# Scanning the products of later retention gates block by block in the recurrence, before the spill

## The chip, the core and the metric

The kernel runs on one core of one Trainium2 chip. The metric is the device time of one execution in microseconds (us). Engines are named as in the profile: PE (TensorE), ACT (ScalarE), DVE (VectorE), POOL (GpSimd) and SP (SyncE, which here only issues DMAs).

## The reference

The input x has 16 batches of 512 time steps and 512 features, all in float32. Four layers are applied in turn, each as `x = x + layer(x)`.

```python
# layer 0: a Haar transform with every coefficient multiplied by the same gate, undone again
gate = sigmoid(silu(cond @ W1.T + b1) @ W2.T + b2)      # [16, 512], from the conditioning input
x = x + (x + x * gate)                                  # what the transform comes to
# layer 1: recurrence over the 512 steps
xw = x @ Wx + b
h[t] = tanh(xw[t] + h[t-1] @ Wh)
x = x + h
# layer 2: gated scan; h0 is the initial hidden state
f, i = sigmoid(x @ W_f.T + b_f), sigmoid(x @ W_i.T + b_i)
g = f / (f + i + EPS) + EPS                             # retention
n = i / (f + i + EPS) * (x @ W_h.T + b_h)               # new information
scaling[t] = g[t] * g[t+1] * ... * g[511]
hidden[t] = sum_{s<=t} scaling[s] * n[s] + g[0] * ... * g[t] * h0
x = x + hidden
# layer 3: a layer of its own for each batch, from the conditioning input
layer[b] = base_layer + x_a[b] @ x_b[b].T               # rank 8
x = x + (x + x @ layer[b])
```

## The kernel before

Features lie on the 128 partitions in four chunks m = 0..3. The kernel has three phases.

**Preamble, 0 to 32 us.** Weights are loaded and split into high and low parts, and the gate of layer 0 and the first block's input products are made.

**Recurrence, 32 to 1103 us.** The 512 steps form 16 blocks j of 32 steps t; a block holds all 16 batches (a tile of 128 x 512 is a chunk of 16 batches x 32 steps). In each step PE multiplies the hidden state by Wh (`step`, L509: 32 matmuls of 128x32 from `hs`, high and low, into the PSUM tile `sums`, which the profile calls recb; the two halves of a sum lie beside each other). DVE adds the halves (L1480, `pre`), ACT takes tanh of `pre` three times (L763 into the fp16 `hs`, L764 into PSUM `konst`, L767 into `hbuf`), and DVE writes the low part of `hs` (L1492), on which the next step of PE waits. Ahead of PE's next accumulation `seed` (L1335, DVE) puts xw of the next step into `sums`: times 1 in one half, times 0 in the other.

Between two steps PE does six matmuls (L545) of the groups: the input product of the next block ("x"), and the gates f, i and the candidate c of the block before. What the other engines do beside the steps is written in tables by step t: `ACT_WORK`, `DVE_EARLY` (between `pre` and the low part of `hs`) and `DVE_LATE` (behind it); in the last block the tables run four steps ahead. In them "x" is the writing of xw (L779), "g" is `forget_share` (L814, retention g into `gst`), "r" a reciprocal of 128x64 (L1295), "p" a forward scan of g (L1325, two halves of 128x264 for a chunk), and "n" the new information into `nst` (L1306). SP spills g (`g_d`), n (`n_d`) and x (`x2_d`) of each block and chunk to HBM, 256 KB each, because the next phase wants them by batch. POOL adds h to x (L1053, L1055) and the share of the initial state (`add_P`, L1068), and divides the gates.

**Tail, 1103 to 1366 us.** First the gate groups of the last block. Then 64 slots k, four chunks m for each batch b. In a slot DVE scans g backwards over the 512 steps (`suffix`, L1527: the scaling), POOL multiplies n by it (`times_n`, L1160), DVE sums that (`hidden`, L1536) and adds it to x (L1539), ACT takes the high part of x (L961) and POOL the low part (`x3_low`, L1167), and PE multiplies them by the base layer (L734). Once a batch PE makes the rank-8 products (L716), ACT takes their high part (L969, L972), POOL the low part (`y_low`, L1172), PE applies them (L749), ACT writes the output rows (`put_out`, L980) and SP stores them. Each engine works through its list in program order; semaphores alone tie them. SP loads g, n and x of a batch two batches ahead, each in halves of 512 KB.

## Time and profile before

| | us |
|---|---|
| median of 3 runs (lowest, highest) | 1370.43 (1368.74, 1372.99) |
| the profiled execution's own time | 1372.59 |
| its span, first to last instruction | 1370.7 |
| steps of the recurrence (511 rows of L1480) | 32.8 to 1102.3 |
| busy PE / DVE / ACT / POOL | 1340.4 / 1066.7 / 695.2 / 767.2 |

The profile lists each instruction with the engine, the line of the kernel, the time it took and the idle time of its engine just before, with what ended it. A slice of the page is a fortieth of the span, 34 us. An engine's busy share says little by itself; the idle time in front of an instruction, and what released it, tell which engine sets the pace at that place.

### The profile page before, as it was taken

The page shows a single profiled execution, that of the slowest core. Times are in us where ns is not written, and L with a number is a line of the kernel's source. Part 1 is how long each engine was busy: PE and PEld are TensorE (multiplying, and loading weights), DVE is VectorE, ACT ScalarE, POOL GpSimd, SP SyncE. Part 2 cuts the span into 40 slices and gives each one's busy share as a digit, 9 for nine tenths or more (in the row PEclk, how much of TensorE's full clock was granted, in tenths as well). Part 3 has the DMA queues.
Part 4 walks back from the last instruction along what each step waited for, and adds up shares of the span by engine and source line. Part 5 has one row for each costly group of instructions (what it writes and reads, how often), then busy time and mean ns, then how long its engine had stood idle before and what let it go on. Part 6 is the DMA issues. An engine that isn't in the chain of part 4 may idle for free. (4 is left out here: it accounts for less than half of the span.)

```text
span 1370.7 us, 50350 instructions
## 1 busy us (share of the span) xinstructions
PE 1340.4 (98%) x21246; PEld 887.3 (65%) x21246; DVE 1066.7 (78%) x2912; ACT 695.2 (51%) x2228; POOL 767.2 (56%) x620
## 2 busy tenths in 40 slices
PE   8999999999999999999999999999999997999998
PEld 6656666666666666666666666666666644677776
DVE  5756878777777777777777787878777888998993
ACT  4388555555555555555555555555545442333332
POOL 3255655464646464545555555554535557887884
PEclk9999999999999999999999999999999998999999
DMA  9771333333434242424242424241416568999993
GB/s 374 271 264 37 64 65 64 64 64 68 69 63 71 57 78 55 74 56 72 56 80 54 81 49 80 48 72 26 71 25 119 143 146 167 330 325 335 329 323 119
DMA packets 442276, 168.13 MB, mean 123 GB/s; under 512 B 406449, under 2 KB 409649, under 8 KB 438850
## 3 DMA queue, kind: packets, MB, share of 16 engines
q1 hardware_dynamic: 441584, 164.53, 47.6%
q8 instruction: 167, 2.74, 0.8%
q14 instruction: 59, 0.48, 0.1%
q10 hardware_dynamic: 466, 0.38, 0.1%
HBM read 96.72 MB, written 68.16 MB: 120 GB/s over the span
## 5 line engine op out<-in xcount | busy, mean ns | idle before, releaser
L509 PEld LDWEIGHTS recb<-hs,scanS 128*128 128x128 f16 x16352 | 466.1, 96 | 148.2 <-DVE hs L1492 144.3
L509 PE MATMUL recb<-hs,scanS 128*128 128x32 f16 x16352 | 488.3, 176 | 4.6 <-DVE hs L1492 3.5
L763 ACT ACTIVATE hs<-pre 128x64 f16<-128x64 f32 x512 | 131.2, 256 | 489.0 <-DVE pre L1480 487.5
L1480 DVE TENSOR_REDUCE pre<-recb 128x64 f32<-128x128 f32 x511 | 148.9, 291 | 186.4 <-PE recb L509 184.3
L1295 DVE RECIPROCAL gates<-gates 128x64 f32<-128x64 f32 (+1 forms) x484 | 257.8, 555 | 0.4
L1053 POOL TENSOR_SCALAR hbuf<-hbuf,sup 128x512 f32<-128x512 f32 (+2 forms) x61 | 94.1, 1542 | 126.9 <-ACT hbuf L767 126.9
L1492 DVE TENSOR_TENSOR hs<-konst,hs 128x64 f16<-128x64 f32 x512 | 103.5, 202 | 61.5 <-ACT konst L764 49.5
L1068 POOL TENSOR_TENSOR xt<-xt,pout 128x512 f32<-128x512 f32 x64 | 75.5, 1179 | 126.4 <-DVE pout L1325 126.4
L1335 DVE TENSOR_TENSOR recb<-xw,recb 128x128 f32<-128x128 f32 x511 | 145.8, 285 | 0.1
L1061 POOL TENSOR_TENSOR gates<-gates 128x512 f32<-128x512 f32 x62 | 78.8, 1271 | 105.0 <-DVE gates L1295 103.7
L767 ACT ACTIVATE hbuf<-pre 128x64 f32<-128x64 f32 x512 | 122.5, 239 | 0.0
L1036 POOL TENSOR_TENSOR x1l<-xt,x1h 128x512 f16<-128x512 f32 x56 | 64.7, 1159 | 93.8 <-ACT x1h L773 93.8
L1055 POOL TENSOR_TENSOR xt<-xt,hbuf 128x512 f32<-128x512 f32 (+1 forms) x65 | 97.9, 1506 | 25.8 <-DVE ratio L1269 17.3
L1167 POOL TENSOR_TENSOR x3l<-xt,x3h 128x512 fp32r<-128x512 f32 x64 | 82.7, 1294 | 45.6 <-ACT x3h L961 42.9
L764 ACT ACTIVATE konst<-pre 128x64 f32<-128x64 f32 x512 | 107.0, 209 | 0.0
L734 PE MATMUL bank<-wx_hi,x3h 128*128 128x512 f32 x208 | 85.5, 411 | 8.0 <-issue 5.1
L545 PE MATMUL bank<-x2l,wc_h 128*128 128x512 f16 x240 | 90.8, 378 | 0.0
L545 PE MATMUL bank<-x2l,wi_h 128*128 128x512 f16 x240 | 90.8, 378 | 0.0
L545 PE MATMUL bank<-x2h,wi_l 128*128 128x512 f16 x240 | 90.7, 378 | 0.0
L545 PE MATMUL bank<-x2h,wc_l 128*128 128x512 f16 x240 | 90.7, 378 | 0.0
L545 PE MATMUL bank<-x2h,wf_l 128*128 128x512 f16 x240 | 90.7, 378 | 0.0
L545 PE MATMUL bank<-x2h,wf_h 128*128 128x512 f16 x240 | 90.5, 377 | 0.0
(252 smaller groups left out, 2725.7 us busy)
## 6 DMA issues: line engine op xcount, KB each, us to landing
xt<-in_x SPq DMA_DIRECT2D x64, 256.0 KB, 3.5
g_d<-gst SPq DMA_DIRECT2D x64, 256.0 KB, 4.2
n_d<-nst SPq DMA_DIRECT2D x64, 256.0 KB, 3.1
x_d<-xt SPq DMA_DIRECT2D x64, 256.0 KB, 3.3
out<-gates SPq DMA_DIRECT2D x63, 256.0 KB, 4.9
xt<-x_d SPq DMA_DIRECT2D x28, 512.0 KB, 6.1
stage<-in_w SPq DMA_DIRECT2D x11, 1024.0 KB, 6.8
xt<-g_d SPq DMA_DIRECT2D x14, 512.0 KB, 8.0
```

Source lines behind the costliest of these rows:

```text
L509: last = nc.tensor.matmul(sums[t % 2][:, m].rearrange("p a b -> p (a b)"), w[:, k, m * P:(m + 1) * P], hs[:, k].rearrange("p a b -> p (a b ...
L545: last = nc.tensor.matmul(bank[n % C][:], w[:, k, m * P:(m + 1) * P], act[:, k, :], start=(e == 0), stop=(e == GM - 1))
L734: last = nc.tensor.matmul(quarter(b, t)[:], x3[q][:, m, tok], w[:, m, :], start=(m == 0 and e == 0), stop=False)
L763: nc.scalar.activation(hs[:, :, 0, :], pre[t % 2][:], ACT.Tanh, scale=unscale).then_inc(s_h, 1)
L764: nc.scalar.activation(hps, pre[t % 2][:], ACT.Tanh, scale=unscale).then_inc(s_h, 1)
L767: nc.scalar.activation(hbuf[:, t % (RING * OCT)], pre[t % 2][:], ACT.Tanh, scale=unscale).then_inc(s_hb, 1)
L1053: nc.gpsimd.tensor_scalar(steps, steps, sup[:, C + j:C + j + 1], None, ALU.mult).then_inc(s_hx, 1)
L1055: last = nc.gpsimd.tensor_tensor(xs, xs, hbuf[:, r + lo:r + hi].rearrange("p t c b -> p c b t"), ALU.add)
L1295: nc.vector.reciprocal(piece, piece).then_inc(s_r, n)
L1335: nc.vector.tensor_tensor(sums[t % 2], gate, keep, ALU.mult)
L1480: nc.vector.tensor_reduce(pre[t % 2][:], sums[t % 2].rearrange("p c a b -> p c b a"), axis=AX.X, op=ALU.add).then_inc(s_pre, 1)
L1492: nc.vector.tensor_tensor(hs[:, :, 1, :], hps, hs[:, :, 0, :], ALU.subtract).then_inc(s_hs, 1)
```

## The change

- g is neither spilled nor loaded any more. Instead DVE scans it backwards within each block while it is in SBUF: `suffix(b, m, e)`, four quarters of 128x132 for each block and chunk (a reset column for each batch), in the steps that `QUARTERS` names.
- POOL multiplies n by that scan before n is spilled (`suffix_share`; `suffix_input`, on the input gate, in the last block). ACT copies each batch's product over the block to `left` (`total_share`, 128x16).
- In the tail DVE scans these totals backwards over the blocks (`following`, four scans of 128x32 for batches 0 and 1, four of 128x224 for the rest; both inputs lie in SBUF), and `times_n` multiplies n by the result, one number for 32 steps (480 columns for batches 0 and 1, else 512). The 64 scans of 512 columns are gone.
- xw is written into `sums` by ACT (`seed`, a copy of 128x128 times 0.5 into both halves), behind the second tanh and ahead of the third, instead of by DVE. PE's step waits for it too (`s_seed`). Two xw writes move one step back in `ACT_WORK`, and two row maxima ("a") from step 9's late list to the early lists of steps 9 and 10.
- The order at the start of the tail is rewritten on DVE, POOL, ACT and SP, and `nst` has four chunks instead of two.

```diff
-ACT_WORK = {1: [("x2h", 0), ("x2h", 1)], 2: [("x2h", 2), ("x2h", 3)], 3: [("x", 0), ("g", 3)], 4: [("x", 1)], 6: [("x", 2)], 8: [("x", 3)],
+ACT_WORK = {1: [("x2h", 0), ("x2h", 1)], 2: [("x2h", 2), ("x2h", 3)], 3: [("g", 3)], 4: [("x", 0)], 5: [("x", 1)], 6: [("x", 2)], 8: [("x", 3)],
...
+             9: [("a", 2)], 10: [("a", 3)], 11: [("zr", 0)], 14: [("r", 0, 0)], 15: [("r", 0, 3)], 16: [("r", 0, 6)], 18: [("r", 1, 0)], 19: [("r", 1, 3)], 20: [("r", 1, 6)],
...
+QUARTERS = {21: [(0, 0)], 22: [(0, 1)], 23: [(0, 2)], 27: [(0, 3)], 28: [(1, 0)], 29: [(1, 1)], 1: [(1, 2)], 2: [(1, 3)],
+            3: [(2, 0)], 4: [(2, 1)], 5: [(2, 2)], 6: [(2, 3)], 7: [(3, 0)], 8: [(3, 1)], 9: [(3, 2), (3, 3)]}
+QUARTERS_LAST = {17: [(0, 0)], 18: [(0, 1)], 19: [(0, 2)], 20: [(0, 3)], 23: [(1, 0)], 24: [(1, 1)], 25: [(1, 2)], 28: [(1, 3)],
+                 29: [(2, 0)], 30: [(2, 1), (2, 2)], 31: [(2, 3)]}
+TOTALS, TOTALS_LAST = {30: 0, 5: 1, 9: 2, 11: 3}, {21: 0, 29: 1, 5: 1, 9: 2, 11: 3}
...
-            def spill_g(b, m):
-                sp.wait_ge(s_g, C * b + m + 1)
-                sp.dma_start(columns(g_d, b, m), gst[:, m, :, 1:SEG]).then_inc(d_g[m], 16)
-
...
+                sp.wait_ge(s_vs if b + 1 < NBLK else s_n, C * b + m + 1)
...
-                    if b:
-                        load("g", b + 2, 0)
-                        load("g", b + 2, 1)
...
                 pe.wait_ge(s_hs, TS * j + t + 1)
+                pe.wait_ge(s_seed, TS * j + t)
...
+            def seed(n):
+                if n == T:
+                    return
+                if n == 1:
+                    act.wait_ge(s_rec, 1)
+                if n % TS == 0:
+                    act.wait_ge(s_xw, C * (n // TS + 1))
+                if n - 1 == BOUND_FIRST:
+                    act.wait_ge(s_bd, 1)
+                elif n - 1 == BOUND_C:
+                    act.wait_ge(s_bd, 9)
+                elif TS < n < T - 2 * TS and (n - 1) % TS == BOUND_STEP:
+                    act.wait_ge(s_bd, 8 * (n // TS + 1) + 1)
+                gate = xw[n // TS % 2][:, n % TS].unsqueeze(2).to_broadcast([P, C, 2, B])
+                nc.scalar.activation(sums[n % 2], gate, ACT.Copy, scale=0.5).then_inc(s_seed, 1)
+
...
+                seed(TS * j + t + 1)
...
-                    act.wait_ge(d_g[m], 16 * b)
+                    act.wait_ge(s_S, 4 * (C * (b - 1) + m + 1))
...
+            def total_share(b, m):
+                act.wait_ge(s_S, 4 * (C * b + m + 1))
+                if b == 1 and m == 0:
+                    act.wait_ge(s_zero, 7)
+                nc.scalar.activation(left[:, m, :, b - 1], sfx[:, m % 2, :, 1], ACT.Copy, scale=sup[:, C - 1:C]).then_inc(s_t, 1)
...
+            def suffix_share(b, m):
+                pool.wait_ge(s_n, C * b + m + 1)
+                pool.wait_ge(s_S, 4 * (C * b + m + 1))
+                info = nst[:, m, :].rearrange("p (b t) -> p b t", t=TS)
+                nc.gpsimd.tensor_tensor(info, info, sfx[:, m % 2, :, 1:SEG], ALU.mult).then_inc(s_vs, 1)
...
-                loaded(pool, "n", k)
-                pool.wait_ge(s_S, k + 1)
-                nc.gpsimd.tensor_tensor(nin[b % 2][:, m, :], nin[b % 2][:, m, :], scan[k % 4], ALU.mult).then_inc(s_u, 1)
+                blocks = NBLK - 1 if b < 2 else NBLK
+                if b < 2:
+                    pool.wait_ge(d_e["n"][b], 32)
+                else:
+                    loaded(pool, "n", k)
+                pool.wait_ge(s_F, m + 1 if b < 2 else C + m + 1)
+                part = nin[b % 2][:, m, 0:blocks * TS].rearrange("p (q t) -> p q t", t=TS)
+                nc.gpsimd.tensor_tensor(part, part, left[:, m, b, 0:blocks].unsqueeze(2).to_broadcast([P, blocks, TS]), ALU.mult).then_inc(s_u, 1)
 
...
+            def suffix_input(m):
+                pool.wait_ge(s_in, C * last + m + 1)
+                pool.wait_ge(s_S, 4 * (C * last + m + 1))
+                share = ivalue(last, m).rearrange("p (b t) -> p b t", t=TS)
+                nc.gpsimd.tensor_tensor(share, share, sfx[:, m % 2, :, 1:SEG], ALU.mult).then_inc(s_iv, 1)
...
-            def seed(j, t):
-                j, t = j + t // TS, t % TS
-                if j == NBLK:
-                    return
-                if t == 0 and j:
-                    dve.wait_ge(s_xw, C * (j + 1))
-                gate = xw[j % 2][:, t].unsqueeze(2).to_broadcast([P, C, 2, B])
-                keep = halves.unsqueeze(1).unsqueeze(3).to_broadcast([P, C, 2, B])
-                nc.vector.tensor_tensor(sums[t % 2], gate, keep, ALU.mult)
+            def suffix(b, m, e):
+                part = slice(e * B // 4, (e + 1) * B // 4)
+                if e == 0:
+                    dve.wait_ge(s_g, C * b + m + 1)
+                    before, chunk = (b, m - 2) if m >= 2 else (b - 1, m + 2)
+                    if before == NBLK - 1:
+                        dve.wait_ge(s_iv, chunk + 1)
+                    elif before >= 0:
+                        dve.wait_ge(s_vs, C * before + chunk + 1)
+                    else:
+                        dve.wait_ge(s_xp, 2 * C)
+                        dve.wait_ge(s_zero, 7)
+                    if before >= 1:
+                        dve.wait_ge(s_t, C * (before - 1) + chunk + 1)
+                dst, src = (s[:, part, :].rearrange("p b t -> p (b t)")[:, ::-1] for s in (sfx[:, m % 2], gst[:, m]))
+                nc.vector.tensor_tensor_scan(dst, src, restart[:, ::-1], inv[:, C - 1:C], ALU.mult, ALU.add).then_inc(s_S, 1)
+
+            def following(m, lo, hi):
+                if lo == 0:
+                    dve.wait_ge(s_t, C * (NBLK - 2) + m + 1)
+                run, begin = (s[:, lo:hi, :].rearrange("p b q -> p (b q)")[:, ::-1] for s in (left[:, m], fresh))
+                nc.vector.tensor_tensor_scan(run, run, begin, 0.0, ALU.mult, ALU.add).then_inc(s_F, 1)
...
-                        dve.wait_ge(s_rec, 1)
-                        nc.vector.memset(halves[:, 0:1], 1.0)
-                        nc.vector.memset(halves[:, 1:2], 0.0).then_inc(s_halves, 1)
-                        dve.wait_ge(s_halves, 1)
...
-                    seed(j, t + 1)
...
-            def suffix(k):
-                b, m = k // C, k % C
-                loaded(dve, "g", k)
-                if k >= 4:
-                    dve.wait_ge(s_u, k - 3)
-                elif k == 0:
-                    dve.wait_ge(s_one2, 2)
-                    dve.wait_ge(s_rec, TS * NBLK)
-                nc.vector.tensor_tensor_scan(scan[k % 4][:, ::-1], gin[b % 2][:, m, ::-1], konst[:, 1:2].to_broadcast([P, T]), inv[:, C - 1:C],
-                                             ALU.mult, ALU.mult).then_inc(s_S, 1)
+                        nc.vector.memset(restart, 0.0).then_inc(s_zero, 1)
...
+            suffix_share(last - 1, 2)
             add_P(last - 1, 1)
+            suffix_share(last - 1, 3)
             add_P(last - 1, 2)
             shares(last, 0)
             add_P(last - 1, 3)
             shares(last, 1)
+            suffix_input(0)
+            shares(last, 2)
+            times_n(0)
+            suffix_input(1)
             add_P(last, 0)
-            shares(last, 2)
             info_share(0)
-            times_n(0)
             shares(last, 3)
             info_share(1)
-            add_P(last, 1)
             times_n(1)
             x3_low(0)
-            add_P(last, 2)
+            add_P(last, 1)
+            suffix_input(2)
             times_n(2)
             x3_low(1)
+            suffix_input(3)
+            add_P(last, 2)
             times_n(3)
+            x3_low(2)
             add_P(last, 3)
-            x3_low(2)
             x3_low(3)
...
             decays(last - 1, 1, 1)
+            whole_suffix(last - 1, 3)
             decays(last - 1, 2)
-            decays(last - 1, 3, 0, 1)
+            decays(last - 1, 3)
             shares_of(0)
-            decays(last - 1, 3, 1)
             shares_of(1)
+            whole_suffix(last, 0)
+            shares_of(2)
+            following(0, 0, 2)
+            whole_suffix(last, 1)
             decays(last, 0)
-            shares_of(2)
-            suffix(0)
             shares_of(3)
+            following(1, 0, 2)
+            whole_suffix(last, 2)
+            hidden(0)
             decays(last, 1)
-            suffix(1)
-            hidden(0)
             dve.wait_ge(s_n, C * last + 2)
             info(2)
-            suffix(2)
+            hidden(1)
+            whole_suffix(last, 3)
+            following(2, 0, 2)
             decays(last, 2)
-            hidden(1)
             info(3)
-            suffix(3)
             hidden(2)
+            following(3, 0, 2)
             decays(last, 3)
             hidden(3)
-            suffix(C)
-            suffix(C + 1)
-            hidden(C)
-            suffix(C + 2)
-            hidden(C + 1)
-            suffix(C + 3)
-            hidden(C + 2)
-            suffix(C + 4)
-            suffix(C + 5)
-            for k in range(C + 3, SLOTS):
-                if k + 3 < SLOTS:
-                    suffix(k + 3)
+            for m in range(C):
+                following(m, 2, B)
+            for k in range(C, SLOTS):
                 hidden(k)
```

ACT, steps 3 to 5 of a middle block, before. `r_s_pre` is the wait for DVE's sum, `u_s_S` (after) that for a backward scan.

```order
L763 ACTIVATE hs<-pre 128x4x16 [waits r_s_pre]
L764 ACTIVATE konst<-pre 128x64
L767 ACTIVATE hbuf<-pre 128x64
L779 ACTIVATE xw<-bank,bias,gscale 128x16x32 [waits v_s_bd,r_s_xp]
L814 ACTIVATE gst<-gates 128x16x32 [waits r_s_P,r_d_g3,r_s_fr]
L763 ACTIVATE hs<-pre 128x4x16 [waits r_s_pre]
```

The same place after:

```order
L764 ACTIVATE hs<-pre 128x4x16 [waits r_s_pre]
L765 ACTIVATE konst<-pre 128x64
L759 ACTIVATE recb<-xw 128x128
L769 ACTIVATE hbuf<-pre 128x64
L817 ACTIVATE gst<-gates 128x16x32 [waits r_s_P,u_s_S,r_s_fr]
L764 ACTIVATE hs<-pre 128x4x16 [waits r_s_pre]
L765 ACTIVATE konst<-pre 128x64
L759 ACTIVATE recb<-xw 128x128
L769 ACTIVATE hbuf<-pre 128x64
L782 ACTIVATE xw<-bank,bias,gscale 128x16x32 [waits v_s_bd,r_s_seed,r_s_xp]
```

A fourth instruction stands in each step, and the write of xw has moved one step back.

POOL, from the last division of gates but one to the second low part of x, before (`late` and `xw` hold n of the tail, `scanS` the backward scan):

```order
L1062 TENSOR_TENSOR gates<-gates 128x512
L1178 TENSOR_TENSOR nst<-nst,gates 128x512 [waits r_s_in,t_s_cb]
L1068 TENSOR_TENSOR xt<-xt,pout 128x512 [waits r_s_lowd,r_s_P]
L1160 TENSOR_TENSOR xw<-xw,scanS 128x512 [waits t_s_S,t_s_nc,t_d_en0]
L1167 TENSOR_TENSOR x3l<-xt,x3h 128x512 [waits t_s_x3h]
L1068 TENSOR_TENSOR xt<-xt,pout 128x512 [waits r_s_lowd,r_s_P]
L1160 TENSOR_TENSOR xw<-xw,scanS 128x512 [waits t_s_S,t_s_nc,t_d_en0]
L1167 TENSOR_TENSOR x3l<-xt,x3h 128x512 [waits t_s_x3h]
```

The same place after (`left` holds the products over the later blocks, `sfx` the scan within the block, `hbuf` the last block's input gate):

```order
L1069 TENSOR_TENSOR gates<-gates 128x512
L1212 TENSOR_TENSOR nst<-nst,gates 128x512 [waits u_s_iv,t_s_cb]
L1188 TENSOR_TENSOR xw<-xw,left 128x480 [waits u_s_F,t_d_en0]
L1195 TENSOR_TENSOR x3l<-xt,x3h 128x512 [waits t_s_x3h]
L1075 TENSOR_TENSOR xt<-xt,pout 128x512 [waits r_s_lowd,r_s_P]
L1207 TENSOR_TENSOR hbuf<-hbuf,sfx 128x512 [waits u_s_S,r_s_in]
L1188 TENSOR_TENSOR xw<-xw,left 128x480 [waits u_s_F,t_d_en0]
L1195 TENSOR_TENSOR x3l<-xt,x3h 128x512 [waits t_s_x3h]
L1207 TENSOR_TENSOR hbuf<-hbuf,sfx 128x512 [waits u_s_S,r_s_in]
L1075 TENSOR_TENSOR xt<-xt,pout 128x512 [waits r_s_lowd,r_s_P]
```

Two multiplies of the last block's input gate (L1207) have come in, each waiting for a backward scan of DVE, and `add_P` now stands behind the low part.

## Rows read from the trace of the kernel before

**Rows 1.** the page's slices of the span, tenths busy; PE, then DMA.

```profile
PE   8999999999999999999999999999999997999998
...
DMA  9771333333434242424242424241416568999993
```

**Rows 2.** timeline of one step: start, us taken, engine, line, [idle before <-releaser].

```profile
501.74 0.95 PE L509 MATMUL recb<-hs,scanS 128*128 128x32 f16 x32
...
502.74 0.29 DVE L1480 TENSOR_REDUCE pre<-recb 128x64 f32<-128x128 f32 x1
...
503.06 0.26 ACT L763 ACTIVATE hs<-pre 128x64 f16<-128x64 f32 x1 [1.55 <-DVE pre L1480]
...
503.37 0.24 ACT L767 ACTIVATE hbuf<-pre 128x64 f32<-128x64 f32 x1
503.47 0.22 DVE L1492 TENSOR_TENSOR hs<-konst,hs 128x64 f16<-128x64 f32 x1 [0.24 <-ACT konst L764]
...
503.84 0.95 PE L509 MATMUL recb<-hs,scanS 128*128 128x32 f16 x32
```

**Rows 3.** timeline of ACT behind an xw write, block 1, step 3.

```profile
106.96 0.26 ACT L763 ACTIVATE hs<-pre 128x64 f16<-128x64 f32 x1
```

**Rows 4.** groups by line: count | busy us, mean ns | idle before.

```profile
L972 ACT COPY xar<-recb 128x128 f32<-128x128 f32 x16 | 4.4, 273 | 0.0
...
L1325 DVE TENSOR_TENSOR_SCAN pout<-gst,spare 128x264 f32<-128x264 f32 x13 | 9.1, 704 | 1.3
...
L1160 POOL TENSOR_TENSOR late<-late,scanS 128x512 f32<-128x512 f32 x32 | 41.4, 1293 | 2.4 <-DVE scanS L1527 2.4
...
L1068 POOL TENSOR_TENSOR xt<-xt,pout 128x512 f32<-128x512 f32 x7 | 8.3, 1180 | 8.3 <-DVE pout L1325 8.3
...
L1055 POOL TENSOR_TENSOR xt<-xt,hbuf 128x512 f32<-128x512 f32 x42 | 64.0, 1524 | 3.5
```

**Rows 5.** timeline of POOL and DVE at 1071 us.

```profile
1071.23 1.53 POOL L1055 TENSOR_TENSOR xt<-xt,hbuf 128x512 f32<-128x512 f32 x1
1071.65 1.26 DVE L1347 SCALAR_TENSOR_TENSOR late<-ident,late 128x128 f32<-128x128 f32 x1
```

**Rows 6.** timeline from the last step to the first output product.

```profile
1103.28 0.60 POOL L1053 TENSOR_SCALAR hbuf<-hbuf,sup 128x128 f32<-128x128 f32 x1 [0.46 <-ACT hbuf L767]
...
1135.46 1.20 DVE L1536 TENSOR_TENSOR_SCAN recb<-konst,xw 128x512 f32<-128x512 f32 x1
...
1145.83 1.21 DVE L1536 TENSOR_TENSOR_SCAN recb<-konst,xw 128x512 f32<-128x512 f32 x1
...
1151.47 0.69 DVE L1539 TENSOR_TENSOR xt<-xt,recb 128x512 f32<-128x512 f32 x1 [0.47 <-ACT xt L944]
...
1161.34 0.46 POOL L1172 TENSOR_TENSOR ys<-xar,ys 128x128 fp32r<-128x128 f32 x1
1161.85 0.74 PE L749 MATMUL bank<-xbt,ys 16*128 16x512 f32 x8 [0.83 <-POOL ys L1172]
```

**Rows 7.** timeline of later batches of the tail, PE, ACT and POOL.

```profile
1244.24 0.50 PE L749 MATMUL bank<-xbt,ys 16*128 16x512 f32 x3
...
1247.81 0.41 PE L716 MATMUL recb<-xt,xa 128*16 128x128 f32 x8 [2.05 <-DVE xt L1539]
...
1299.99 0.74 PE L749 MATMUL bank<-xbt,ys 16*128 16x512 f32 x8 [0.21 <-POOL ys L1172]
...
1300.77 2.42 ACT L980 ACTIVATE gates<-bank,itok 128x512 f32<-128x512 f32 x4 [7.33 <-PE bank L749]
...
1303.77 1.30 POOL L1167 TENSOR_TENSOR x3l<-xt,x3h 128x512 fp32r<-128x512 f32 x1 [2.59 <-ACT x3h L961]
...
1313.03 0.50 PE L749 MATMUL spare<-xbt,ys 16*128 16x512 f32 x1 [0.18 <-POOL ys L1172]
...
1351.92 0.50 PE L749 MATMUL bank<-xbt,ys 16*128 16x512 f32 x3
...
1364.70 0.74 PE L749 MATMUL bank<-xbt,ys 16*128 16x512 f32 x8
```

More of the change, by code:

```diff
@@ L202, in build @@
         xlast = xt[(NBLK - 1) % XT]
-        scan = [scanS[k // 2][:, k % 2, :] for k in range(4)]
         oout = gates[:, 0:NT]
@@ L1001, in _ @@
             last_X(1)
+            total_share(last, 3)
             last_n(2)
@@ L1147, in _ @@
             base_low(2)
+            suffix_share(j - 1, 0)
             shares(j - 1, 2)
```

186 lines of the change are left out of this document (100 added, 86 removed), and 2 rows, old and new, of the table DVE_LATE.

## The prediction

> **What bounds the kernel now.** I read the page's slices first: PE is at 9 tenths in 37 of 40, and the two slices at 7 lie where the recurrence ends and the tail begins; the DMA engines are near 9 tenths only in the tail [rows 1]. Then three stretches, each by its timeline.
>
> In the recurrence a step is one loop [rows 2]: PE's 32 small matmuls start at 501.74, DVE adds the halves at 502.74, ACT's first tanh starts at 503.06, the low part of hs is written at 503.47, and PE goes on at 503.84, 2.10 us after the start. But PE shows no idle time there: it fills the gap with its six large matmuls, and the low part (ended 503.69) is 0.15 us early. The 512 steps are PE's: whatever DVE or ACT gains inside a step is worth nothing, and the first 0.15 us of a loss cost nothing.
>
> At the start of the tail nothing is full: DVE, POOL and ACT hand each other work from the last step (1103.28) to the first output product of PE (1161.85), 58 us, with idle time on every engine [rows 6].
>
> In the steady tail a batch takes 13.04 us (1299.99, the product before, to 1313.03). The loop is: output product, ACT writes four output rows (1300.77), ACT's high part, POOL's first low part of x of the batch (1303.77, released by ACT), four more low parts and three multiplies by n at 1.25 us each, `y_low`, output product (1313.03, released by `y_low`) [rows 7]. PE's own floor is 12.78 (1351.92 to 1364.70, where the others have run out of work). So POOL costs 0.27 us a batch over the floor. Once, between 1244.24 and 1260.84, a batch took 16.6: PE's rank-8 product waited 2.05 us for DVE's sum [rows 7].
>
> **The change, recurrence.** The seed leaves DVE and goes to ACT. It was already hidden, so its removal gives nothing. On ACT it starts when the third tanh does now, 503.37, that is 0.63 after the sum's start at 502.74. Its nearest row is the 128x128 copy out of PSUM, 273 ns [rows 4]; it ends about 0.90 after the sum. The low part ends at 0.95. So the seed is ready 0.05 before what PE waits for anyway, and 0.2 before PE is free. Cost nothing; the cover is those 0.2 us, and if the seed took twice as long, 0.55, it would end at 1.18, 0.08 a step too late, 41 us in all: that is a rival. ACT has 1.55 us idle before its next tanh in such a step [rows 2]. Only where ACT is full, as behind the xw writes of block 1 (no idle time before the tanh) [rows 3] and at two steps of block 0, the 0.15 to 0.3 us more lands on the step: six steps, some 0.8 us. The backward scans of 128x132 take half of a 128x264 scan, 0.35 us [rows 4], in steps where DVE has 0.4 to 0.5 idle once the seed is gone. Some memsets in block 1 add 0.3. Spills of g vanish, POOL's 64 multiplies (1.25) fill its idle time. **Recurrence: +1.1 us** (bounds 0 and +3).
>
> **The start of the tail.** I carried every instruction from the last step to the second output product through the four new orders, each at the pitch of its row before, with 0.08 for a semaphore; the old orders came out within 0.2 us of the trace. What moves, in order:
> - POOL multiplies the 15th block's third chunk of n (1.25) before it adds the last h; 0.46 was idle [rows 6], so all that follows is 0.8 later.
> - DVE now has a whole backward scan (4 x 0.34 = 1.36) and a 264-column scan (1.0 with its carry) ahead of the first gate sum: 2.9 later. Three more whole scans (4.1) against two scans of 512 columns less (2.5) stand before the first hidden sum: 1135.5 becomes 1138.2, +2.7 [rows 6].
> - Second: the new information of chunk 2 now waits for POOL's multiply of the input gate, which stands behind `add_P` and the first low part: the second hidden sum is 4.1 later.
> - Third: ACT's high part of chunk 1 now stands behind `total_share` of chunk 3, which waits for DVE's last whole scan (ends 1149.4), so it comes at 1149.9, 5.8 later. POOL waits for it, and only then multiplies the input gate of chunk 3 (1152.0), for which DVE's information (1153.4) and hidden sum 2 wait: 1145.8 becomes 1154.0, +8.2. This is the largest term.
> - The fourth x sum moves from 1151.5 to 1160.3 [rows 6]. Four `following` scans of 224 columns come ahead of the next hidden sum, 0.55 each, against five scans of 512 columns (1.2 each) less; some waiting for POOL is in there, below.
> - POOL's `y_low` moves from 1161.3 to 1169.5, and the first output product from 1161.85 to 1170.0: **+8.1 us.**
>
> The second output product follows 16.7 later as before: POOL's list between them is the same.
>
> **The steady tail.** DVE loses its 512-column scan, some 3.1 us a slot down to 1.9; before, it was 12.4 of 13.05 a batch. The 2.05 us wait on DVE must vanish, and with it the long batch: 16.6 - 13.1 = **-3.5 us** [rows 7]. POOL's loop stays: n times a broadcast is one multiply of 512 columns as before. Loads fall from 4 MB a batch to 3; no load was on this loop. What the multiply costs decides the rate. Nearest is the same multiply with a scan as its second input, 1293 ns; `add_P`, whose second input is strided by 33 columns in blocks, 1180; the add of h, strided by 64 elements, 1524 [rows 4]. I take 1293, since line and shapes are the same but for the second input. At 1180, 0.11 x 3 = 0.34 a batch, the loop falls to PE's floor: -0.27 x 12 batches = -3.3, and -1.2 at the start. At 1524, 0.23 more for each of three multiplies is 0.7 a batch, 9.0 in 13 batches, and eight of them in the start add 1.8 to 2.5: 5.7 + 11.3 = +17.
>
> The Trainium skill speaks to this too (GPSIMD Engine Reference, "Performance pitfalls for Q7 kernels"): reads whose element step is over 8 bytes cost about 1.5 times. The 1524 against 1180 agree in direction; by it a broadcast, of step zero, would not pay.
>
> **Two engines at SBUF.** DVE's product of two SBUF tiles started at 1071.65, while POOL's add from 1071.23 ran, and took 1.26 us [rows 5]; the same line took 0.28 the other three times. It ended at 1072.91, 0.15 behind POOL's add. `following` reads both inputs in SBUF, so I have counted that each of the last two waits for one POOL instruction, 1.2 in all, within the 8.1.
>
> The Trainium skill (SBUF - State Buffer, "SBUF: two separate sides") calls that pair of ports an exclusive lock, whichever starts first. The row agrees with it. If POOL issued back to back and never let go, the four scans would wait out POOL's list; by the skill alone I can't tell how often.
>
> **Sum.** +1.1 + 8.1 - 3.5 = +5.7. Of the profiled execution, 1372.59, this makes 1378.3; its span 1376.4. The median of the runs is 1370.43, 2.2 below the profiled one; so **1376 us**. Own range +3 to +8.5, 1373.5 to 1379.
>
> **The rivals.**
> - **Multiply at the cheap price.** POOL falls under PE's floor: 5.7 - 4.5 = +1.2 to +2, 1372. For it: the second input is 16 numbers. Against: 1293 is the price of most POOL multiplies here.
> - **Multiply at the strided price, or starved scans.** +17, 1387, if an operand in four dimensions is addressed as slowly as the add of h; or, if `following` waits through six POOL instructions of 1.25, 5.7 + 7.5, 1383. For the first speaks that the tile is cut in blocks of 32, against it that `add_P`'s is too.
> - **The seed sets the step: slower.** One mechanism: ACT's write into `sums` ends after the low part of hs. The place is each of 510 steps; 10 ns over cost 5 us. It decides from an end 1.10 us after the sum's start (0.95 + 0.15); I have 0.90. ACT's row of 128x128 reads PSUM and writes SBUF, the seed the other way round. 1386 to 1400.
> - **Faster.** The start of the tail slips by under 3.5 us, because semaphores and POOL's waits are less strict than my chain, and the long batch goes with some of the rate: +1.1 + 3 - 3.5 - 4.5 = -4 to -7, 1364 to 1366. Against: the chain through the third hidden sum stands in program order on three engines.
> - **It doesn't do what it says:** the long batch of 16.6 comes from elsewhere (a transfer) and stays: +9.2, 1379.6. DVE was idle there for a load, but PE's wait names the sum. It is within the forecast's case.
>
> **How the numbers follow.** Forecast, 50%. Cheap multiply 18%, dear multiply or starved scans 11%, seed 7%, faster 14%. This kernel's measurement can tell 0.3%, 4.1 us: 1366.3 and 1374.5. Of the forecast's 50, 15 lie below 1374.5, so same is 15 + 18 = 33; slower 35 + 18 = 53; faster 14. The likeliest is 1376. The range reaches down to 1365, taking in half of the faster case, and up to 1388, the dear multiply; outside are some 7 below, and 7 to 9 above (most of the seed's case and the tail of the starved scans).
>
> **What the profile after would show.** Steps of 2.10 with PE never idle in front of L509 but in blocks 0 and 1: the seed is hidden; idle time there released by ACT's recb: it isn't. The first L749 at 1170 against 1161.85, the third hidden sum 8 later than 1145.8, released by POOL: the start is right. One batch after another at 13.05 with no 16.6: the rest is. The multiply by `left` is at 1.29, 1.18 or 1.52. I am wrong above all if the third hidden sum isn't late, or if PE waits for ACT in the steps.

## The result, and the profile after

The changed kernel takes 1375.63 us (median of 8 runs, 1375.14 to 1377.71) against 1370.33 before (8 runs, 1368.74 to 1372.99): ratio 1.0040, 95% interval 1.0031 to 1.0049, 5.3 us slower. The two profiled executions lie closer: 1372.59 before, 1375.69 after.

By the traces the 3.1 us between them come about like this (sums are the DVE sums L1480/L1531, output products the PE products L749/L734):

| stretch, us | before | after | change |
|---|---|---|---|
| start to first sum | 32.8 | 33.3 | +0.5 |
| first to last sum of the recurrence | 1069.5 | 1072.1 | +2.6 |
| last sum to first output product | 59.5 | 66.5 | +6.9 |
| first to second output product | 16.7 | 15.6 | -1.2 |
| second to last output product | 186.1 | 180.4 | -5.7 |

The page's slices after, which answer to [rows 1]:

```profile
PE   8999999999999999999999999999999996999998
...
DMA  9771131414131313232223223130305344777773
```

The DMA engines fell from 9 tenths to 7 in the tail; PE has one slice at 6 where the tail begins.

A step of a middle block after, the timeline of PE, DVE and ACT that answers to [rows 2]:

```profile
504.19 0.95 PE L493 MATMUL recb<-hs,scanS 128*128 128x32 f16 x32
...
505.18 0.29 DVE L1531 TENSOR_REDUCE pre<-recb 128x64 f32<-128x128 f32 x1
...
505.50 0.26 ACT L764 ACTIVATE hs<-pre 128x64 f16<-128x64 f32 x1 [1.35 <-DVE pre L1531]
...
505.81 0.26 ACT L759 ACTIVATE recb<-xw 128x128 f32<-128x128 f32 x1
505.91 0.22 DVE L1542 TENSOR_TENSOR hs<-konst,hs 128x64 f16<-128x64 f32 x1 [0.44 <-ACT konst L765]
...
506.28 0.95 PE L493 MATMUL recb<-hs,scanS 128*128 128x32 f16 x32
```

Still 2.09 us a step. The seed (L759, 0.26 us) starts 0.63 after the sum's start and ends at 506.07. The low part of hs ends at 506.13, and PE goes on at 506.28. So the seed is hidden: it is done 0.06 before the low part and 0.2 before PE goes on.

The start of the tail, timelines of POOL, DVE, ACT and PE, against [rows 6]:

```profile
1106.79 0.60 POOL L1060 TENSOR_SCALAR hbuf<-hbuf,sup 128x128 f32<-128x128 f32 x1
...
1141.26 1.21 DVE L1593 TENSOR_TENSOR_SCAN recb<-konst,xw 128x512 f32<-128x512 f32 x1
...
1152.48 0.32 ACT L823 ACTIVATE left<-sfx,sup 128x16 f32<-128x16 f32 x1 [5.20 <-DVE sfx L1384]
...
1152.70 0.99 POOL L1188 TENSOR_TENSOR xw<-xw,left 128x480 f32<-128x480 f32 x1 [4.65 <-DVE left L1390]
...
1153.65 1.26 POOL L1195 TENSOR_TENSOR x3l<-xt,x3h 128x512 fp32r<-128x512 f32 x1
...
1156.18 0.75 DVE L1348 SCALAR_TENSOR_TENSOR nst<-bank,cbias,hbuf 128x512 f32<-128x512 f32 x1 [1.63 <-POOL hbuf L1207]
1156.85 1.22 DVE L1593 TENSOR_TENSOR_SCAN recb<-konst,xw 128x512 f32<-128x512 f32 x1
...
1162.88 0.69 DVE L1596 TENSOR_TENSOR xt<-xt,recb 128x512 f32<-128x512 f32 x1 [0.74 <-ACT xt L947]
1163.49 3.97 DVE L1390 TENSOR_TENSOR_SCAN left<-left,fresh 128x224 f32<-128x224 f32 x4
...
1171.36 0.45 POOL L1200 TENSOR_TENSOR ys<-xar,ys 128x128 fp32r<-128x128 f32 x1
1171.86 0.74 PE L734 MATMUL bank<-xbt,ys 16*128 16x512 f32 x8 [1.82 <-POOL ys L1200]
```

ACT's high part of chunk 1 stood behind `total_share` (L823), ahead of which ACT was idle 5.20 us for DVE's last whole scan. POOL stood there too: its multiply of n for chunk 2 (1152.70) waited 4.65 us for the short scan that DVE makes behind the same whole scan, and its low part of chunk 1 (1153.65) followed without a gap. Then came the multiply of the input gate, for which DVE's information of chunk 3 (L1348) waited, and behind that the third hidden sum (1156.85, before 1145.83). The four scans of 224 columns (1163.49) took 3.97.

The later batches, groups by line of POOL and the timeline of two output products of PE, against [rows 4, 7]:

```profile
L1188 POOL TENSOR_TENSOR late<-late,left 128x512 f32<-128x512 f32 x28 | 29.5, 1052 | 0.0
...
1252.89 0.50 PE L734 MATMUL bank<-xbt,ys 16*128 16x512 f32 x3
...
1265.66 0.49 PE L734 MATMUL bank<-xbt,ys 16*128 16x512 f32 x1
```

The multiply takes 1052 ns, before 1293, and a batch 12.77, which before only the last two batches reached: PE's floor. All batches from the sixth on are at it, and none is long.

### The profile page after: what moved, and what is told of

Same layout as the page of the kernel before. It is cut to its first block and busy times, and to the rows that moved or that the text cites. A ratio compares the mean times of both kernels' runs of the same rounds, so it can differ in the third digit from the quotient of the medians.

```text
span 1373.9 us, 51141 instructions
## 1 busy us (share of the span) xinstructions
PE 1340.4 (98%) x21246; PEld 898.3 (65%) x21246; DVE 1018.9 (74%) x2604; ACT 807.8 (59%) x2791; POOL 824.3 (60%) x684
## 5 line engine op out<-in xcount | busy, mean ns | idle before, releaser
L493 PEld LDWEIGHTS recb<-hs,scanS 128*128 128x128 f16 x16352 | 477.7, 96 | 138.4 <-DVE hs L1542 134.4
L1531 DVE TENSOR_REDUCE pre<-recb 128x64 f32<-128x128 f32 x511 | 148.9, 291 | 123.3 <-PE recb L493 98.5
L1542 DVE TENSOR_TENSOR hs<-konst,hs 128x64 f16<-128x64 f32 x512 | 114.9, 224 | 117.7 <-ACT konst L765 117.7
L759 ACT ACTIVATE recb<-xw 128x128 f32<-128x128 f32 x511 | 133.7, 262 | 0.0
L1075 POOL TENSOR_TENSOR xt<-xt,pout 128x512 f32<-128x512 f32 x64 | 75.6, 1181 | 73.4 <-DVE pout L1367 73.3
L1384 DVE TENSOR_TENSOR_SCAN sfx<-gst,inv,spare 128x132 f32<-128x132 f32 x256 | 117.8, 470 | 0.0
L1195 POOL TENSOR_TENSOR x3l<-xt,x3h 128x512 fp32r<-128x512 f32 x64 | 82.7, 1293 | 54.5 <-ACT x3h L962 54.5
```

The costliest lines, as they stand in the source:

```text
L493: last = nc.tensor.matmul(sums[t % 2][:, m].rearrange("p a b -> p (a b)"), w[:, k, m * P:(m + 1) * P], hs[:, k].rearrange("p a b -> p (a b ...
L759: nc.scalar.activation(sums[n % 2], gate, ACT.Copy, scale=0.5).then_inc(s_seed, 1)
L1384: nc.vector.tensor_tensor_scan(dst, src, restart[:, ::-1], inv[:, C - 1:C], ALU.mult, ALU.add).then_inc(s_S, 1)
L1531: nc.vector.tensor_reduce(pre[t % 2][:], sums[t % 2].rearrange("p c a b -> p c b a"), axis=AX.X, op=ALU.add).then_inc(s_pre, 1)
L1542: nc.vector.tensor_tensor(hs[:, :, 1, :], hps, hs[:, :, 0, :], ALU.subtract).then_inc(s_hs, 1)
```

## The experiments

Medians, ratios to before with their intervals, and the stretches of the table above in the profiled execution of each. Each ratio is taken to executions of the kernel before made beside that kernel; their medians lie from 1370.14 to 1371.05, so a ratio doesn't follow exactly from the first row:

| kernel | us | ratio | recurrence | last sum to first product | first to second | second to last |
|---|---|---|---|---|---|---|
| before | 1370.33 | | 1069.5 | 59.5 | 16.7 | 186.1 |
| before_again | 1369.85 (one) | | 1068.4 | 59.6 | 17.3 | 183.8 |
| after | 1375.63 | 1.0040 (1.0031 to 1.0049) | 1072.1 | 66.5 | 15.6 | 180.4 |
| b_bcast | 1367.69 | 0.9981 (0.9971 to 0.9991) | 1068.8 | 58.9 | 16.3 | 182.3 |
| b_no_g_load | 1369.57 | 0.9995 (0.9985 to 1.0005) | 1069.6 | 59.6 | 16.7 | 182.6 |
| b_seed_act | 1373.13 | 1.0013 (1.0004 to 1.0021) | 1073.6 | 59.5 | 16.7 | 182.9 |
| a_dense | 1380.00 | 1.0070 (1.0053 to 1.0087) | 1071.7 | 66.5 | 16.7 | 182.5 |
| a_fresh_psum | 1375.47 | 1.0033 (1.0024 to 1.0042) | 1071.8 | 65.9 | 15.6 | 180.4 |
| a_seed_dve | 1378.72 | 1.0057 (1.0045 to 1.0069) | 1074.3 | 66.5 | 15.7 | 180.6 |
| a_seed_two | 1374.21 | 1.0027 (1.0016 to 1.0038) | 1070.4 | 66.5 | 15.9 | 180.5 |
| a_start_order | 1369.83 | 1.0000 (0.9990 to 1.0010) | 1072.8 | 61.0 | 15.9 | 180.4 |
| a_order_muls | 1369.49 | 0.9987 (0.9979 to 0.9996) | 1071.8 | 59.8 | 15.9 | 180.4 |
| a_best | 1367.92 | 0.9974 (0.9965 to 0.9984) | 1071.6 | 61.0 | 13.5 | 180.4 |
| a_best_two | 1367.92 | 0.9982 (0.9973 to 0.9991) | 1072.4 | 59.8 | 15.2 | 180.4 |

### What the multiply costs: b_bcast and a_dense

On the kernel before:

```diff
-                nc.gpsimd.tensor_tensor(nin[b % 2][:, m, :], nin[b % 2][:, m, :], scan[k % 4], ALU.mult).then_inc(s_u, 1)
+                part = nin[b % 2][:, m, :].rearrange("p (q t) -> p q t", t=TS)
+                nc.gpsimd.tensor_tensor(part, part, scan[k % 4][:, 0:NBLK].unsqueeze(2).to_broadcast([P, NBLK, TS]), ALU.mult).then_inc(s_u, 1)
```

> The kernel before, with one edit: POOL's multiply of n in the tail takes as second input 16 columns of the scan, each spread over 32, instead of all 512 (so the scaling is left out of the result); scans, loads and waits stay. Theory M (the price of the multiply puts POOL's loop under PE's floor): the multiply takes 1.05 us instead of 1.29, a late batch 12.8 instead of 13.05, and from the first to the second output product 15.5 instead of 16.7: 3 to 4 us less in all, about 1367. Rival R (the rate after came from DVE's room or from fewer loads): multiply cheaper, but batches stay at 13.05 and the total within 1 us of before.

On the changed kernel:

```diff
+                if b >= 2:
+                    share = left[:, m % 2:m % 2 + 2].rearrange("p c b q -> p (c b q)").rearrange("p (q t) -> p q t", t=TS)
```

> The changed kernel, with one edit: for batches 2 to 15 POOL's multiply of n reads 512 columns one after another instead of 16 spread over 32 (the scaling is wrong in the result). Theory M: the multiply takes 1.29 instead of 1.05, late batches 13.05 instead of 12.77, nine of them 2.5 us, and 0.7 to 1 us more from the first to the second output product: 1379 against 1375.6. Rival R: batches stay at 12.77, the total within 1 us of the changed kernel.

The multiply in each, groups by line of POOL, first of b_bcast, then of a_dense:

```profile
L1161 POOL TENSOR_TENSOR late<-late,scanS 128x512 f32<-128x512 f32 x26 | 27.3, 1050 | 0.0
```

```profile
L1191 POOL TENSOR_TENSOR late<-late,left 128x512 f32<-128x512 f32 x28 | 36.2, 1292 | 0.0
```

1050 and 1292 ns: the price goes with the way the second input is read, in both kernels, whichever tile holds it. With the cheap one the kernel before had its later batches at 12.77 (but one, 14.65), with all its scans and loads; with the dear one the changed kernel had 13.01 to 13.05 and took 4.4 us more. Theory M holds in both directions, R falls. Of the 4.4 us the stretches of a_dense show 3.2: 2.0 in the later batches and 1.2 between the first two products; the rest lies outside them. In b_bcast the first two products came only 0.4 nearer to each other, not the 1.2 expected: there ACT waited 2.5 to 3.4 us for each of DVE's sums, and DVE still had its 512-column scans.

### The long batch: b_no_g_load and before_again

```diff
-                    if b:
-                        load("g", b + 2, 0)
-                        load("g", b + 2, 1)
```

> The kernel before, without the loads of g for batches 3 to 15: DVE scans the g of earlier batches again (wrong scaling), as long as before. Theory L (the one batch of 16.6 us comes from the loads, 4 MB in and out in 13 us at a DMA share of 1.0): no such batch, all late ones at 13.05, total 3.5 us less in executions that have it. Rival V (it comes from DVE, busy 12.4 of 13.05 us, which falls behind by itself): the long batch stays.

> The kernel before, unchanged, for the length of its long batch in another execution. The profiled one had one batch of 16.6 us and lay 2.2 us over the median of the runs; the other kernels with all loads of g had 14.65 and 13.33 in its place. If the loads decide it by chance of an execution, it is between 13.0 and 15 here, and the execution nearer to the median; if it belongs to the order of the work, 16.6 again.

Ahead of the long batch of the kernel before, its timeline of DVE shows a wait that I had not quoted; and the windows of that batch before, and of the same batch of b_no_g_load (length, busy time of PE, PEld, DVE, ACT and POOL, granted clock, DMA share, GB/s):

```profile
1238.35 1.28 DVE L1527 TENSOR_TENSOR_SCAN scanS<-xt,inv,konst 128x512 f32<-128x512 f32 x1 [3.67 <-DMA xt<-g_d]
```

```profile
1244.20:1260.80 16.60, 14.51 (x88) 11.08 (x88) 16.08 (x17) 5.02 (x10) 11.63 (x10) 0.90 1.01 355
```

```profile
1244.20:1257.20 13.00, 12.84 (x88) 10.02 (x88) 12.58 (x14) 4.92 (x10) 10.42 (x10) 1.00 0.76 265
```

DVE waited 3.67 us for g from HBM, in a stretch in which the DMA engines were full (share 1.01, 355 GB/s); then it ran its scans one after another, and PE waited for its sum. Without g's loads the share is 0.76 and all batches are at 13.02 to 13.05. In b_bcast's long batch DVE waited for g too, 2.63 us. So the cause is the load, with DVE's 12.4 of 13.05 leaving no room to catch up. But how long it gets is chance of an execution: 16.6, 14.65 (b_bcast), 13.33 (b_seed_act), and in before_again 14.2 one batch earlier, where PE waited 1.23 us:

```profile
1233.63 0.41 PE L716 MATMUL recb<-xt,xa 128*16 128x128 f32 x8 [1.23 <-DVE xt L1539]
```

In the median this is little: b_no_g_load is 0.6 us faster than the kernel before beside it, within its interval. The profiled execution of before, 2.3 us over the median, was one of the bad ones.

### The seed: b_seed_act, a_seed_dve, a_seed_two

b_seed_act is the kernel before with the changed kernel's `seed` on ACT. a_seed_dve is the changed kernel with DVE's seed:

```diff
+SEED_DVE = range(1, T)
...
-                if n == T:
+                if n == T or n in SEED_DVE:
...
                         nc.vector.tensor_reduce(pre[t % 2][:], sums[t % 2].rearrange("p c a b -> p c b a"), axis=AX.X, op=ALU.add).then_inc(s_pre, 1)
+                    seed_dve(TS * j + t + 1)
```

a_seed_two has `[n for n in range(1, T) if n % TS not in (10, 11)]` instead.

> The kernel before with the seed alone moved to ACT. If the seed on ACT is what made the recurrence 3.1 us longer (and not the scans): blocks 0 and 1 longer by 1.1 and 0.5, the tail unchanged, total 1.5 to 2.5 us more than before, 1372. If the scans or the memsets did: within 0.5 us of before. If the seed reached PE in each step: 10 us or more.

> The changed kernel with the seed back on DVE, right behind the sum, everything else as changed. Theory W (on DVE the seed lies where DVE waits for ACT's second tanh anyway, 0.44 us in the changed trace, so it buys no room for the scans; on ACT it costs where ACT is full): blocks 0 to 2 lose what they gained, the recurrence is 1.5 to 2 us shorter than the changed kernel's, total 1374. Rival N (the seed had to leave for the backward scans to fit in DVE's steps): the steps with a scan of 128x132 become 0.1 to 0.2 us longer, 15 in a block, 20 to 40 us in all.

> The changed kernel with the seeds back on DVE except the two of a block that stand beside a row maximum (those issued in steps 9 and 10), which stay on ACT. The run with every seed on DVE showed 0.18 us more in exactly these two steps of each block and none in the steps with a scan. Theory X (only the maxima, put ahead of the low part of hs, need the seed gone; the scans don't): middle blocks at 67.06, block 0 at 64.9 instead of 66.55, total 1.5 us under the changed kernel, 1374. Rival Y (a seed on DVE costs elsewhere too, by some waits between engines): blocks over 67.2, total 1376 or more.

b_seed_act is 2.1 us slower than the kernel before beside it (1371.05). Its block 1 takes 67.47 (before 67.07, after 67.53), in four or five steps of 0.1 each. In block 0 three steps are 0.17 to 0.24 longer (7, 21 and 26, some 0.6 together), in b_seed_act and in all kernels with that block's seeds on ACT, and in none with them on DVE. A step of the last block (17) adds 0.2, and each middle block 0.05 in b_seed_act alone. Its profiled recurrence is 4.1 us longer, but 2.2 of that are one step of block 0 (28), in which PE waited 1.37 us for a weight.

The length of block 0 as a whole proves less: 64.3 to 66.0 with DVE's seed in seven executions, 66.3 to 67.6 with ACT's in six, but 67.5 with DVE's in a_best_two. Two other things in it go by the execution. TensorE's granted clock was at the lower of its two levels (1.2 instead of 2.4 GHz) around steps 2 to 4 in some executions and not in others; these three steps took 7.17 us before and 6.36 in before_again. The windows of that stretch, before and in before_again (columns as above; the clock is the third number from the end):

```profile
33.50:36.80 3.30, 3.30 (x39) 2.15 (x38) 2.92 (x9) 1.26 (x6) 0.28 (x1) 0.50 1.05 420
```

```profile
33.70:37.00 3.30, 3.24 (x71) 2.35 (x69) 2.97 (x9) 1.29 (x6) 0.43 (x1) 1.00 1.06 423
```

And late in the block PE waits for the load of a weight, 0.36 to 1.56 us where it waits; timeline of PE in a_best_two:

```profile
96.81 1.06 PE L543 MATMUL spare<-stage,hgT 128*32 128x512 f32 x8 [1.56 <-DMA stage<-in_w]
```

Block 2 is not the seed's. It is 0.3 longer in every changed kernel, with the seed on DVE as well (67.38 in a_seed_two), and 67.12 in b_seed_act. The timeline of DVE after shows why, ahead of the sum of its step 2: a quarter scan stands between the information and a row maximum, and the sum comes 0.4 late.

```profile
170.39 0.74 DVE L1348 SCALAR_TENSOR_TENSOR nst<-bank,cbias,gates 128x512 f32<-128x512 f32 x1
171.05 0.48 DVE L1384 TENSOR_TENSOR_SCAN sfx<-gst,inv,spare 128x132 f32<-128x132 f32 x1
171.45 0.67 DVE L1270 TENSOR_REDUCE amax<-xt 128x1 bf16<-128x512 f32 x1
172.02 0.28 DVE L1531 TENSOR_REDUCE pre<-recb 128x64 f32<-128x128 f32 x1
```

Steps 10 and 31 of the last block are 0.2 longer each in the same way, behind two quarter scans.

In a_seed_dve I was wrong: block 0 fell to 64.9, but each middle block rose from 67.06 to 67.42, and the kernel is 3.1 us slower than the changed one. It is two steps of the 32, by 0.18 each. The timeline of DVE in the first of them:

```profile
387.06 0.28 DVE L1378 TENSOR_TENSOR recb<-xw,recb 128x128 f32<-128x128 f32 x1
387.25 0.68 DVE L1272 TENSOR_REDUCE amax<-xt 128x1 bf16<-128x512 f32 x1
387.85 0.22 DVE L1558 TENSOR_TENSOR hs<-konst,hs 128x64 f16<-128x64 f32 x1
```

The change had put a row maximum (0.68) ahead of the low part of hs; with the seed ahead of it too the low part starts 1.00 after the sum instead of 0.80. With those two seeds on ACT and all others on DVE (a_seed_two) the middle blocks are at 67.06 again, with the scans in them. The scans did not need the seed gone: before, a step still had 0.24 us of idle time on DVE ahead of the low part with the seed there, and 0.44 without it. Only the two maxima that had been moved to make room for scans needed it. a_seed_two is 1.4 us under the changed kernel.

### Two inputs in SBUF: a_fresh_psum

```diff
-                run, begin = (s[:, lo:hi, :].rearrange("p b q -> p (b q)")[:, ::-1] for s in (left[:, m], fresh))
+                run, begin = (s[:, lo:hi, :].rearrange("p b q -> p (b q)")[:, ::-1] for s in (left[:, m], fresh if lo == 0 else aux[:, 0:B * NBLK].rearrange("p (b q) -> p b q", q=NBLK)))
```

> The changed kernel, with the second input of the four long scans of the block totals (the pattern of zeros and ones) in PSUM instead of SBUF, written by DVE ahead of the first hidden sum. Theory P (with two inputs in SBUF such a scan waits for POOL's running instruction): the four take 2.2 us together instead of 4.0, starting without delay; the second output product and the total 1 to 1.8 us earlier, 1374. Rival Q (a scan of this form is that slow): still 4.0 us for the four, total unchanged.

```profile
1163.12 2.15 DVE L1395 TENSOR_TENSOR_SCAN left<-left,aux 128x224 f32<-128x224 f32 x4
```

2.15 us for the four scans (596 ns each) instead of 3.97: with both inputs in SBUF two of them took 1.65 and 1.35, each ending 0.5 behind the end of a POOL instruction, 1.8 us in all. POOL waited as well: its first two multiplies of 480 columns beside them took 1.31 us each, and 0.99 here. But the first output product came only 0.6 earlier, and the median is not clearly lower (1375.47): DVE then waited 1.00 for POOL, which had become the later one. So theory P holds for the scans, and the 1 to 1.8 us in the total did not come.

### The order at the start of the tail: a_start_order, a_order_muls, a_best

On DVE (a_start_order; POOL does `suffix_input(2)` ahead of `times_n(1)`, `add_P(last, 1)` ahead of `x3_low(0)`, `suffix_input(3)` ahead of `times_n(2)`, `times_n(3)` ahead of `add_P(last, 2)` and `y_low(0)` ahead of `x3_low(C)`, ACT `total_share(last, 3)` ahead of `last_X(1)`):

```diff
             hidden(0)
             decays(last, 1)
+            whole_suffix(last, 3)
+            following(2, 0, 2)
             dve.wait_ge(s_n, C * last + 2)
             info(2)
             hidden(1)
-            whole_suffix(last, 3)
-            following(2, 0, 2)
-            decays(last, 2)
+            following(3, 0, 2)
             info(3)
+            decays(last, 2)
             hidden(2)
-            following(3, 0, 2)
             decays(last, 3)
             hidden(3)
-            for m in range(C):
-                following(m, 2, B)
+            hidden(C)
+            following(0, 2, B)
+            hidden(C + 1)
...
```

> The changed kernel with the start of the tail in another order: DVE's last whole scan and the short scans of chunks 2 and 3 ahead of the new information, both multiplies of the input gate early on POOL, the low part of y ahead of that of x, and the long scans of the block totals between the next hidden sums. Theory S (the start is late through the chain last whole scan, total, high part, input gate, information of chunk 3, on which PE's first batch waits): information of chunk 3 at 1150 instead of 1156.2, first output product near 1164 instead of 1171.9, total 7 to 8 us less, 1368. Rival T (PE, slower there at its lower clock, or waits at SBUF set it): first output product at 1169 or later, total at most 3 us less.

DVE's information of chunk 3 in a_start_order, then POOL's first low part of slot 5 and ACT's output rows in a_order_muls:

```profile
1152.54 0.73 DVE L1348 SCALAR_TENSOR_TENSOR nst<-bank,cbias,hbuf 128x512 f32<-128x512 f32 x1
```

```profile
1166.88 1.84 ACT L981 ACTIVATE gates<-bank,itok 128x512 f32<-128x512 f32 x3 [2.99 <-PE bank L734]
...
1169.89 1.62 POOL L1195 TENSOR_TENSOR x3l<-xt,x3h 128x512 fp32r<-128x512 f32 x1 [2.92 <-ACT x3h L962]
```

The stretch from last sum to first product fell by 5.4 us, and the median by 5.8, to that of before. Counted from the last sum, the information of chunk 3 is 5.5 us earlier. So what the change lost at the start of the tail was the order, and the chain to the information of chunk 3 is where most of it sat. Three engines' orders were changed at once, so no run tells its links apart. Of the 7 to 8 us that I expected a part did not come: now PE's own products for the first batch came last, back to back but for the rank-8 ones up to the first output product, and part of them at the lower clock (below).

a_order_muls puts `times_n(C)` behind `add_P(last, 2)` and `times_n(C + 1)` behind `add_P(last, 3)`.

> The reordered kernel, with POOL's multiplies of n for the first two chunks of batch 1 put into its two idle stretches of 1.76 us, ahead of the low parts of x of chunks 2 and 3, instead of behind them. Theory: the hidden sum of slot 4 no longer waits 3.0 us for POOL, the first output product stays (PE's own work sets it), the second comes 13.2 to 14 us behind it instead of 15.85: total 2 to 2.7 us less than the reordered kernel's 1369.8, that is 1367.5. Rival: PE's output rows on ACT set the distance, total unchanged.

The median is 0.3 us under that of a_start_order, not 2 to 2.7: the rival holds. The distance of the second product stayed at 15.9. ACT wrote four output rows (2.42 us) ahead of slot 5's high part, and POOL waited 2.92 for that. The first product came 1.3 us earlier, but no run shows that the edit did it. The windows of PE from 53.4 to 56.7 us after the last sum show another cause, in a_start_order, a_order_muls, a_best and a_best_two (length, busy time of PE, granted clock, DMA share, GB/s):

```profile
1160.60:1163.90 3.30, 3.30 (x9) 0.51 0.36 82
```

```profile
1159.80:1163.10 3.30, 3.08 (x42) 1.00 0.34 87
```

```profile
1158.60:1161.90 3.30, 3.30 (x10) 0.50 0.34 86
```

```profile
1159.10:1162.40 3.30, 3.15 (x42) 1.00 0.36 85
```

Where the granted clock was 0.5 there (its lower level, 1.2 of 2.4 GHz), a product of 128x512 took 0.63 us instead of 0.39, and the first output product came 61.0 after the last sum; where it was 1.0, it came at 59.7 and 59.8. a_best and a_best_two have the same order there and lie on either side. PE had stood idle 1.7 to 2.1 us just ahead of these products in all four.

So in a_best, which also has the seeds of blocks 0 and 1 on DVE:

```diff
             x3_high(C)
+            x3_high(C + 1)
             for t in range(NT):
                 put_out(0, t)
-            for k in range(C + 1, 2 * C):
+            for k in range(C + 2, 2 * C):
```

> The kernel with the reordered start and the early multiplies, with two edits more: ACT takes the high part of x of slot 5 ahead of its four output rows of batch 0, and the seeds of blocks 0 and 1 are on DVE. Theory: the low part of x of slot 5, 2.9 us late for ACT's output rows, comes 2.8 earlier, the second output product 13.1 to 13.6 us behind the first instead of 15.9; blocks 0 to 1 1.6 shorter; total 4 less than the 1369.5 of the kernel it is made from: 1365.3, 0.4% under before. Rival: PE's products or the rank-8 chain hold the second batch, only the 1.6 come: 1368.

```profile
1165.30 0.62 ACT L964 CAST x3h<-xt 128x512 fp32r<-128x512 f32 x1 [0.99 <-DVE xt L1614]
1166.93 1.84 ACT L983 ACTIVATE gates<-bank,itok 128x512 f32<-128x512 f32 x3 [1.01 <-PE bank L736]
...
1179.67 0.49 PE L736 MATMUL spare<-xbt,ys 16*128 16x512 f32 x1 [0.17 <-POOL ys L1203]
```

The high part now stands ahead of the rows, and the second product comes 13.5 us behind the first. 1367.92, 2.4 us under before and 7.7 under the changed kernel: this beats both, but it is the rival's 1368 and not the 1365.3 expected. In its execution the first product came 1.2 us later than in a_order_muls, by the clock as shown above, so the second came only 1.1 earlier counted from the last sum (74.5 against 75.6). And block 1 still took 67.48: the seeds of steps 10 and 11, beside the row maxima, were on DVE too.

> The last reordered kernel, with the seeds on DVE in every block but for the two beside the row maxima (instead of in blocks 0 and 1 alone). From the two runs that it joins: block 1 at 67.1 instead of 67.5, the rest as there, 0.5 to 1 us less than 1367.9, that is 1367.2. If the seeds on DVE cost something that the single run hid: 1368.5 or more.

The same median, 1367.92. Block 1 is at 67.1 as expected, but block 0 took 67.5 in its execution, with 1.56 us of PE's wait for a weight. The two first products lie 15.2 apart where the same order gave 13.5, but the first came 1.2 earlier, with the clock up: counted from the last sum the second comes at 75.0 against 74.5. Inconclusive between the two: what is left differs by less than executions do.

## Why the prediction was right, and where it was not

The time, 1375.63 against 1376, and the sign were right. That the time is so close is luck: four terms were off by 1 to 3.4 us each, and their errors cancelled.

- **Middle blocks: right.** 2.09 to 2.10 a step, blocks 3 to 14 within 0.1 of before, the seed ended 0.89 after the sum's start against 0.90.
- **Recurrence, +1.1: too small, +3.1** in the traces with the start. The mechanism named (ACT is full there) is shown by b_seed_act and a_seed_two for about 1.3 of it: three steps of block 0, block 1 and a step of the last block. Another 0.6 is one that the prediction had priced at nothing: the quarter scans, on DVE, in a step of block 2 and two of the last block. They had been taken at half of a 264-column scan, 0.35 us, in steps with room for them; they took 0.47. The start (+0.5; 32.8 to 34.6 over all executions) and 0.4 to 0.5 of block 0 are within what executions of one kernel differ by. 0.2 in other blocks stays open.
- **Start of the tail, +8.1: +6.9.** From the last sum, the first gate sum came 2.8 later (2.9 in the prediction, with POOL's 0.8), the first hidden sum 2.7 (2.7), the second 3.7 (4.1), the third 7.9 (8.2), the fourth x sum 8.3 (8.8). So 0.5 of the 1.2 was gone by then and 0.7 came behind it; the cheaper multiply stands there, but no run tells its part. One link was another than named: POOL waited for DVE's short scan behind the last whole scan (4.65 us), not for ACT's high part, which was ready 0.1 before POOL got to it. a_start_order took most of the loss back with orders alone.
- **The multiply: the step that failed.** The prediction took 1293 ns, between rows of 1180 and 1524, and gave the cheap case 18%. It was 1052, under both of its bounds. None of the rows of before had a spread operand, so the lower bound ought to have been open. By it the rate went to PE's floor as the first rival said.
- **The long batch, -3.5: -3.5 between the traces (16.60 against 13.05), but not between the medians.** It vanished, as said. The term was read from one execution that lay 2.2 us over the median, and I carried it to the median whole; b_no_g_load puts it at 0.6 there. And the cause was a load of g, which the prediction named only as what would keep the batch long.
- **The wait at SBUF: right in kind**, 1.8 us against 1.2, by a_fresh_psum; only 0.6 of it reached the first product.
- **Not doing what it says; seed late; strided price:** none came.

Two rows were misread, without effect on the sum: the page before has one slice of PE at 7 and two at 8, not two at 7, and POOL's loop has three more low parts behind the first, not four.

In the medians, as an estimate from these stretches: the recurrence was 1.0 too small, the start 1.2 too large, 3.2 to 3.4 of multiply was not counted, and 2.9 of long batch was counted that the median does not have. That makes 5.0 to 5.2 us in place of the 5.7 forecast; 5.3 were measured.

## What to carry to other kernels

Work that is taken out of a loop gains only what it held back there, and is paid where it lands. Here the 64 long scans left a steady tail in which DVE still kept pace; what replaced them was hidden in most steps of the recurrence but not at the start of the tail, where nothing was full and each engine waited for the next. What counted there was the order, 5.4 us by the order alone. The gain in the steady tail came from the multiply, which the change made cheaper without aiming at it. Before a term is read from a rare event in a profile, the distance of that execution from the median says how much of it the median holds. Before a shift of 1 us between two traces is put down to an edit, the granted clock of that stretch is to be compared. And an engine's idle time can lie where the work that it is to give room to doesn't go: the seed filled a wait that came back when it left.

## What the runs showed of the hardware that I had not expected

- POOL's multiply of 128x512 takes 1050 to 1052 ns when its second input is 16 numbers spread over 32 columns each, 1292 when it is 512 numbers (b_bcast, a_dense, after): 0.24 us less for the same output.
- A DVE scan of 128x224 with both inputs in SBUF took up to 1.65 us beside POOL's low parts and multiplies, 596 ns with one in PSUM (after, a_fresh_psum). The wait goes both ways: POOL's multiplies of 480 columns took 1.31 us beside such scans and 0.99 beside the others.
- The Trainium skill (SBUF - State Buffer, "SBUF: two separate sides") has the pair of ports as a lock that one of the two engines holds for a whole instruction, if a DVE instruction has both inputs in SBUF. The trace agrees: each of the two delayed scans ended 0.5 us behind the end of a POOL instruction.
- The 128x132 scans took 471 ns each in the recurrence, two thirds of a 128x264 scan (695) rather than half; back to back they started 0.38 us apart (after).
- With TensorE's granted clock at 0.5 (1.2 instead of 2.4 GHz) a product of 128x512 float32 took 0.63 us, at 1.0 it took 0.39. Whether a stretch had it went by the execution: at 33.5 us before had it and before_again did not. At the first output product it was worth 1.2 us (a_best 61.0 after the last sum, a_best_two 59.8).
